# A graph layer with attention: later segment sums, earlier attention and a written-out end on TensorE

## The chip, the cores and the metric

The kernel runs on one core of a Trainium2 chip. The metric is device time of one execution in microseconds. Three executions of the kernel before took 1295.53, 1297.51 and 1299.25 us (median 1297.51). The engines are called PE (TensorE, matrix products), DVE (VectorE), ACT (ScalarE), POOL (GpSimd) and SP (SyncE, here only a queue for transfers). Each engine works through its own list of instructions in order; semaphores tie the lists together.

## What is computed

All numbers are 32-bit floats. There are 8192 nodes with 256 channels and 131072 edges, sorted by target node; the edges have 64 features.

```
ea  = edge_attr @ w_e + b_e
agg = segment_sum(relu(x[src] + ea), dst)            # the edge part
h_local = bn1(relu((x + agg) @ w1 + b1) @ w2 + b2 + x)
q, k, v = split(x @ in_w.T + in_b)                   # attention inside groups of 32 nodes, 4 heads
h_attn  = bn2(softmax(q k^T / 8) v @ out_w.T + out_b + x)
out = h_local + h_attn
out = bn3(out + relu(out @ m_w1 + m_b1) @ m_w2 + m_b2)
result = layernorm(x + out)
```

## The kernel before

The work is laid out in 264 turns, and every engine's list is written turn by turn (in each engine's block, `for turn in range(TURNS)`). Three strands run side by side.

**Edges.** An edge tile has 128 edges, a pair two tiles, a group four pairs; there are 128 groups, two turns each. For a pair POOL gathers two tiles of source rows from DRAM into one of seven slots `xg` (two indirect DMAs, L430); 14 of the 512 pairs are fetched row by row through the queues of SP and ACT instead. DVE adds the edge bias and puts the rows into one of four accumulator banks (`seed`, L681), PE adds the edge product (`products`, L867, two pairs a turn), ACT takes the relu (`message`, L469). For a group PE then sums the messages with one-hot matrices (`sum_group`, L882), ACT copies the sums (`copy_agg`, L474), PE transposes them (`transpose_agg`, L891) and DVE adds them to the 64 columns of `aggT` that belong to the group (`add_agg`, L714, four dependent adds). In DVE's list a turn begins with the seeds of the next turn's products; what stands later in the list delays the seeds of the turn after.

**Attention.** Sixteen slabs J of 512 nodes. `HEADS` and `heads_base(J)` give the turns: q and k products, scores in two halves (`sc`: PE L938, then on DVE four maxima L726 and four differences L731), the softmax halves (`soft`: exp on ACT, then DVE L738 to L747), v, and the product with v (`av`).

**Nodes.** Blocks b of nodes: twelve of 512, six of 256 (12 to 17), four of 128 (18 to 21). `NODES`, `NODES_256` and `NODES_128` give the turns of the stages w1, B (out_w and w2 in one bank), m1, m2, T (transposes back to rows, then on DVE the add of x, L779, and the statistics, L783 and L787) and y (the normalization, L792 to L803). The first 512-node block starts at turn 19, the next ones 16 turns apart. w1 of a block waits on PE until DVE has read the last T of the block before (`s_r`).

The functions that the change touches:

Of the kernel before, what the change touches and what calls it, by code (L numbers as in the profile page):

```python
# [15 lines left out]
CC = C // 128  # L16
P = 128
TG = 8
GE = TG * P
NG = E // GE  # L20
# [37 lines left out]


def heads_base(J):  # L60
    return max(16 * J - 12, 12 * J)

# [5 lines left out]
         "T": (14, 15), "log": (15, 16), "y": (16, 17), "xn": (8, 9), "out": (17, 18)}  # L68
NODES_256 = {"w1": (0,), "B": (1,), "z": (2,), "m1": (2, 3), "m2": (4,), "T": (5,), "log": (6,),
             "y": (7,), "xn": (2,), "out": (8,)}  # L70
FIRST_256 = {12: 211, 13: 217, 14: 223, 15: 229, 16: 235, 17: 243}
NODES_128 = {
# [8 lines left out]
}  # L81
LASTB = 21


SUMS = {2 * n + 1: n for n in range(NG)}
TURNS = 264
CHUNKS = {"w1": CC, "B": CC, "m1": 2 * CC, "m2": CC}

# [36 lines left out]
def nodes_in(turn, stages):  # L125
    found = []
    for b in range(len(BLOCKS)):
        if b < 12:
            plan, base = NODES, 16 * b + 19
        elif b < 18:  # L130
            plan, base = NODES_256, FIRST_256[b]
        else:
            plan, base = NODES_128[b], 0
        found += [(b, s, n) for s in stages for n, at in enumerate(plan[s]) if base + at == turn]
    return found
# [89 lines left out]
def program(nc, k):  # L225
# [3 lines left out]
    with ExitStack() as ctx:  # L229
# [88 lines left out]
        def _(sp):  # L318
# [44 lines left out]
            for turn in range(TURNS):  # L363
# [4 lines left out]
                    preload(i + AHEAD)  # L368
                if turn in (2, 12):
                    load_xT(1 if turn == 2 else 2)  # L370
                if turn % 16 == 13 and NXT <= (turn + 19) // 16 < NJ:
                    load_xT((turn + 19) // 16)
                for J, _, pair in heads_in(turn - 1, ("av",)):
                    sp.wait_ge(s_oc, 2 * J + pair + 1)
                    sp.dma_start(k.oT_dram[2 * J + pair, :, :, :],
# [458 lines left out]
        def _(pe):  # L834
# [134 lines left out]

            def node(b, stage, use):  # L970
                n0, w = BLOCKS[b]
                at, to = cols(b), bank(b, stage)
                J, of_slab = part(b)
                if stage == "w1":
                    if use:
                        pe.wait_ge(s_h1, before(b, "w1") + use)
                    else:
                        if b == 0:
                            pe.wait_ge(s_w1, 16)
                            pe.wait_ge(s_bias, 1)  # L980
                        elif b < 18:
                            pe.wait_ge(s_r, before(b, "T"))
                        elif b == 18:
                            pe.wait_ge(s_oc, 2 * NJ)
                        elif b < LASTB:
                            pe.wait_ge(s_r, before(b - 1, "T"))
                        pe.wait_ge(s_added, min((n0 + w) // PER + SLACK, NG))
                    for c, of in chunks(b, "w1", use):
                        ins = product(to[:, of], CC, lambda a: k.w1[:, a, c * P:(c + 1) * P],
                                      lambda a: aggT[:, a, n0:n0 + w])  # L990
                    ins.then_inc(s_p1, 1)
                if stage == "B":
                    early = b == LASTB
                    if use:
                        pe.wait_ge(s_o, before(b, "B") + use)
                    else:
                        pe.wait_ge(s_oc, (n0 + w + NB - 1) // NB)
                    if early:
                        for c, of in chunks(b, "B", use):
                            product(to[:, of], CC, lambda a: k.owT[:, a, c * P:(c + 1) * P],  # L1000
                                    lambda a: k.oT[:, J % NOT, a, of_slab], start=c == 0,
                                    stop=False, skip=True)
                    if not use:
                        pe.wait_ge(s_h1, before(b + 1, "w1"))
                    for c, of in chunks(b, "B", use):
                        if not early:
                            product(to[:, of], CC, lambda a: k.owT[:, a, c * P:(c + 1) * P],
                                    lambda a: k.oT[:, J % NOT, a, of_slab], stop=False)
                        ins = product(to[:, of], CC, lambda a: k.w2[:, a, c * P:(c + 1) * P],
                                      lambda a: k.h1[:, a, at], start=False, skip=early)  # L1010
                    ins.then_inc(s_p2, 1)
# [27 lines left out]
                                                      k.z[:, c, row:row + P], ident[:, :])  # L1039
                    ins.then_inc(s_t, 1)  # L1040

            for turn in range(TURNS):
                if turn < ND:
                    products(turn)
                if turn - 1 in SUMS:
                    transpose_agg(SUMS[turn - 1])
                weights(turn)
# [1 line left out]
                    attention(J, stage, n)  # L1049
                for b, stage, use in nodes_in(turn, ("T", "m2", "m1", "B", "w1")):  # L1050
                    node(b, stage, use)
                if turn in SUMS:
                    sum_group(SUMS[turn])
            with pe.If(pe.value_load(k.bad_i[0:1, 0:1], min_val=0, max_val=1) > 0):
                pe.wait_ge(s_go, 1)
                general_tensor(nc, k, g, pe)
# [309 lines left out]
```

## Time and profile before

| | |
|---|---|
| median of three executions | 1297.51 us |
| the profiled execution | 1296.03 us, of which 1294.2 us lie between its first and last instruction |
| PE / DVE / ACT / POOL busy | 89% / 64% / 42% / 73% |
| granted clock of PE, mean | 0.969 of full speed |

A busy share is an average over the span. POOL's 73% is low only because the time between two gathers does not count as busy. The chain of work that ended last runs over PE for 58% of the span, DVE for 11%, POOL for 6%.

### The profile page before, as it was taken

To read this page: it belongs to the slowest core of one execution; us is meant where nothing else is said; L and a number is where in the kernel's file an instruction comes from. 1 tells how busy PE (TensorE), PEld (TensorE's weight loads), DVE (VectorE), ACT (ScalarE), POOL (GpSimd) and SP (SyncE) were. 2 spreads that over 40 slices of the span, in tenths; PEclk is the share of its full clock that TensorE was granted. 3 is DMA by queue.
4 is the path that set the end of the run, shared out by engine and by line. 5 is a ranking of instruction groups with operands and counts; after the bars stand their busy time and mean duration, and the time that the engine had idled before them with its cause. 6 is when DMAs were issued, how large, how long until landed. Compare 5 with 4: busy or idle time off the path is not lost.

```text
span 1294.2 us, 28246 instructions
## 1 busy us (share of the span) xinstructions
PE 1154.5 (89%) x7309; PEld 647.4 (50%) x7309; DVE 826.7 (64%) x2090; ACT 541.2 (42%) x1077; POOL 944.9 (73%) x1004
## 2 busy tenths in 40 slices
PE   6787989998899899998989999998989998998896
PEld 3444454544445444444544545454444555765675
DVE  5847486767566576755758666575756667557563
ACT  1343434444344435434344443443434443443353
POOL 7777777777777777777777777777777777675770
PEclk7898999999999999999999999999999998999999
DMA  8554555655555555565555555555655565554550
GB/s 316 154 170 141 175 156 175 174 173 180 170 165 169 164 182 172 160 183 148 183 173 175 165 165 176 166 175 174 172 164 154 183 183 147 168 160 126 175 155 26
DMA packets 119282, 216.50 MB, mean 167 GB/s; under 512 B 24784, under 2 KB 69584, under 8 KB 119120
## 3 DMA queue, kind: packets, MB, share of 16 engines
q0 software_dynamic: 47808, 130.61, 35.0%
q1 hardware_dynamic: 67312, 79.47, 19.6%
q10 hardware_dynamic: 4000, 4.61, 1.0%
q8 instruction: 59, 0.97, 0.3%
q14 instruction: 103, 0.84, 0.2%
HBM read 197.82 MB, written 16.78 MB: 166 GB/s over the span
## 4 chain that ended last, share of the span: by engine, by line
PE 58%; DVE 11%; ACTq 8%; ACT 7%; issue 7%; POOL 6%; DMA 2%; DVEq 0%; SPq 0%
PE bank L837 33%; PE bank L867 12%; PE bank L882 7%; POOL xg L430 6%; ACTq L463 6%; ACT msg L469 4%; DVE bank L681 3%; PE bank L891 3%; ACTq L311 2%; DVE dif L731 2%; DVE mx L726 2%; PE bank L938 1%; DMA xT<-in_xT_dram 1%; DVE aggT L714 1%; ACT kbd L490 1%
## 5 line engine op out<-in xcount | busy, mean ns | idle before, releaser
L430 POOL DMA_INDIRECT xg<-in_x_dram,srcs x996 | 944.0, 948 | 317.4 <-issue 290.0
L469 ACT ACTIVATE msg<-bank 128x512 f32<-128x512 f32 x512 | 277.8, 595 | 543.6 <-PE bank L867 286.7
L681 DVE TENSOR_TENSOR bank<-xg,bank 128x512 f32<-128x512 f32 x498 | 327.4, 690 | 138.1 <-DMA xg<-in_x_dram,srcs 93.0
L867 PE MATMUL bank<-we,ea 64*128 64x256 f32 x2048 | 301.7, 415 | 35.5 <-DVE bank L681 35.5
L867 PEld LDWEIGHTS bank<-we,ea 64*128 64x128 f32 x2048 | 183.1, 192 | 179.7 <-issue 124.1
L714 DVE TENSOR_TENSOR aggT<-bank,aggT 128x64 f32 x512 | 115.2, 225 | 169.1 <-PE bank L891 115.2
L882 PE MATMUL bank<-msg,onehot 128*32 128x256 f32 x2048 | 141.1, 394 | 49.0 <-ACT msg L469 48.4
L837 PE MATMUL bank<-xT,iwT 128*128 128x512 f32 x256 | 128.2, 624 | 7.6 <-DMA xT<-in_xT_dram 4.0
L837 PE MATMUL bank<-o,m 128*128 128x512 f32 (+2 forms) x352 | 125.6, 491 | 4.6 <-DVE o L758 4.4
L882 PEld LDWEIGHTS bank<-msg,onehot 128*32 128x32 f32 x2048 | 54.4, 111 | 141.6 <-ACT msg L469 96.9
L837 PE MATMUL bank<-h,m 128*128 128x512 f32 (+2 forms) x352 | 116.6, 479 | 2.1 <-ACT h L529 2.1
L837 PEld LDWEIGHTS bank<-o,m 128*128 128x128 f32 x352 | 60.7, 193 | 41.3 <-issue 27.9
L837 PEld LDWEIGHTS bank<-h,m 128*128 128x128 f32 x352 | 60.0, 190 | 41.3 <-issue 34.9
L837 PE MATMUL bank<-aggT,w 128*128 128x512 f32 (+2 forms) x176 | 66.1, 510 | 15.7 <-DVE xn L779 13.8
L474 ACT COPY agg<-bank 128x256 f32<-128x256 f32 x128 | 47.5, 371 | 70.8 <-PE bank L882 67.2
L837 PEld LDWEIGHTS bank<-xT,iwT 128*128 128x128 f32 x256 | 45.4, 198 | 51.9 <-issue 46.0
L767 DVE TENSOR_TENSOR z<-bank,z 128x512 f32<-128x512 f32 (+2 forms) x44 | 23.1, 543 | 72.1 <-PE bank L837 71.9
L891 PE MATMUL bank<-ident,agg 128*128 128x128 f32 x256 | 57.7, 308 | 7.5 <-ACT agg L474 7.5
L837 PE MATMUL bank<-iwT,xT 128*128 128x256 f32 x256 | 64.3, 395 | 0.0
L837 PE MATMUL bank<-oT,owT 128*128 128x512 f32 (+2 forms) x176 | 63.6, 485 | 0.0
L529 ACT ACTIVATE h<-bank,mb 128x512 f32<-128x512 f32 (+2 forms) x88 | 47.5, 570 | 37.3 <-PE bank L837 36.9
L837 PE MATMUL bank<-h,w 128*128 128x512 f32 (+2 forms) x176 | 62.1, 476 | 0.0
(92 smaller groups left out, 938.9 us busy)
## 6 DMA issues: line engine op xcount, KB each, us to landing
rows<-in_x_dram SPq DMA_DIRECT2D x2304, 1.0 KB
ea<-in_ea_dram SPq DMA_DIRECT2D x128, 256.0 KB
rows<-in_x_dram ACTq DMA_DIRECT2D x1280, 1.0 KB
xg<-in_x_dram,srcs POOLq DMA_INDIRECT x996
xT<-in_xT_dram SPq DMA_DIRECT2D x32, 256.0 KB, 4.2
aggT<-in_xT_dram SPq DMA_DIRECT2D x32, 256.0 KB, 4.0
oT_dram<-oT SPq DMA_DIRECT2D x32, 256.0 KB
xn<-in_x_dram SPq DMA_DIRECT2D x32, 256.0 KB
```

The source lines that it names most:

```text
L311: _, of = nc.values_load_multi_w_load_instructions(k.of_rows[at:at + 1, col:col + LOADED], engines=(engine,), min_val=0, max_val=(N - 1) * ...
L430: pool.indirect_dma_start(xg[:, slot % NX, n * C:(n + 1) * C], None, t["x"], bass.IndirectOffsetOnAxis(k.srcs[:, at:at + 1], 0)).then_inc( ...
L463: act.dma_start(row_bytes[e:e + 1, row_buffer(n), two * 4 * C:(two + 1) * 4 * C], x_bytes[0:1, bass.ds(of_row[0][i % LOADED], 4 * C)]).the ...
L469: nc.scalar.activation(msg[:, q % NM, :], EA[q % 4][:, :], ACT.Relu).then_inc(s_msg, 1)
L474: nc.scalar.copy(k.agg[:, :], G[:, 0:C]).then_inc(s_agg, 1)
L529: ins = nc.scalar.activation(k.h2[:, c, at], bank(b, "m1")[:, of], ACT.Relu, bias=k.mb1[:, c:c + 1])
L681: nc.vector.tensor_tensor(EA[q % 4][:, :].rearrange("p (a c) -> p a c", a=2), pair.rearrange("p (a c) -> p a c", a=2), KB[:, 0:C].unsqueez ...
L714: nc.vector.tensor_tensor(window, sums[:, :, sub * W:(sub + 1) * W], window, ALU.add).then_inc(s_added if sub == SUB - 1 else s_part, 1)
L837: ins = nc.tensor.matmul(to, stationary(c), moving(c), start=start and c == 0, stop=stop and c == blocks - 1, skip_group_check=skip)
L867: ins = nc.tensor.matmul(EA[(2 * d + pair) % 4][:, two * C:(two + 1) * C], ea[rows, n % NEA, at:at + P], k.we[rows, :], start=False, stop= ...
L882: ins = nc.tensor.matmul(G[sub * W:(sub + 1) * W, 0:C], onehot[:, n % 2, at, :], msg[:, q % NM, two * C:(two + 1) * C], start=tile == 0, s ...
L891: ins = nc.tensor.transpose(G[:, c * P:(c + 1) * P], k.agg[:, c * P:(c + 1) * P], ident[:, :])
```

## The change

Four things are done.

1. `SUMS`: the sums of groups 0 to 113 move from the end of PE's turn 2n+1 to turn 2n+2, right behind that turn's edge products. The copy on ACT, the transposes on PE and the add on DVE follow a turn later than before. The 512-node blocks and blocks 12 to 16 start one turn later.
2. `heads_base`: attention of slabs 6 to 15 starts five turns sooner, that of slab 4 two and that of slab 5 four turns sooner. The loads of xT are issued at turn 16J-22 instead of 16J-19.
3. The last stages of blocks 19 to 21 are put on other turns on ACT and DVE, and PE's list from turn 254 on is written out.
4. The out_w half of B of block 20 becomes a step of its own ("A"), as it already was for block 21.

```diff
 def heads_base(J):
-    return max(16 * J - 12, 12 * J)
+    return max(16 * J - 17, 12 * J if J < 3 else 14 * J - 6)
...
-FIRST_256 = {12: 211, 13: 217, 14: 223, 15: 229, 16: 235, 17: 243}
+FIRST_256 = {12: 212, 13: 218, 14: 224, 15: 230, 16: 236, 17: 243}
...
+LAST_TURN = 254
...
-SUMS = {2 * n + 1: n for n in range(NG)}
+CLOSE = NG - 14
+SUMS = {(2 * n + 2 if n < CLOSE else 2 * n + 1): n for n in range(NG)}
...
-            plan, base = NODES, 16 * b + 19
+            plan, base = NODES, 16 * b + 20
...
-                if turn % 16 == 13 and NXT <= (turn + 19) // 16 < NJ:
-                    load_xT((turn + 19) // 16)
+                if turn % 16 == 10 and NXT <= (turn + 22) // 16 < NJ:
+                    load_xT((turn + 22) // 16)
...
-            for turn in range(TURNS):
-                if turn < ND:
-                    products(turn)
+            for turn in range(LAST_TURN):
+                products(turn)
+                if SUMS.get(turn, NG) < CLOSE:
+                    sum_group(SUMS[turn])
                 if turn - 1 in SUMS:
                     transpose_agg(SUMS[turn - 1])
...
-                if turn in SUMS:
+                if SUMS.get(turn, 0) >= CLOSE:
                     sum_group(SUMS[turn])
+
+            products(ND - 2)
+            transpose_agg(NG - 2)
+            node(19, "T", 0)
+            products(ND - 1)
+            node(20, "w1", 0)
+            sum_group(NG - 1)
+            node(20, "A", 0)
+            transpose_agg(NG - 1)
+            node(20, "B", 0)
+            node(LASTB, "A", 0)
+            node(LASTB, "w1", 0)
+            node(20, "m1", 0)
+            node(LASTB, "B", 0)
+            node(LASTB, "m1", 0)
+            node(20, "m2", 0)
+            node(LASTB, "m2", 0)
+            node(20, "T", 0)
+            node(LASTB, "T", 0)
```

DVE's list in the kernel before, from the first half of the scores of slab 7 (mx and dif; o is stage B of a node block, sm to probT the softmax):

```order
L726 TENSOR_REDUCE mx<-bank 32x8 x4
L731 TENSOR_TENSOR dif<-bank,mx 32x256 x4
L758 SCALAR_TENSOR_TENSOR o<-xT,s,bank 128x512
L681 TENSOR_TENSOR bank<-xg,bank 128x512 x2
L690 TENSOR_TENSOR onehot<-bank,rel 128x256
L738 TENSOR_REDUCE sm<-dif 128x8
L740 RECIPROCAL rs<-sm 128x8
L742 TENSOR_TENSOR dif<-dif,rs 128x256
L747 STREAM_TRANSPOSE probT<-dif 32x8x32 x4
```

The same place after, up to the first instruction of the normalization (lines are two higher; xn, stats and mv are stage T, fix is stage y):

```order
L728 TENSOR_REDUCE mx<-bank 32x8 x4
L733 TENSOR_TENSOR dif<-bank,mx 32x256 x4
L781 TENSOR_TENSOR xn<-bank,xn 128x512
L785 BN_STATS stats<-xn 128x6 x2
L789 BN_AGGR mv<-stats 128x2 x2
L683 TENSOR_TENSOR bank<-xg,bank 128x512
L683 TENSOR_TENSOR bank<-rows,bank 128x512
L740 TENSOR_REDUCE sm<-dif 128x8
L742 RECIPROCAL rs<-sm 128x8
L744 TENSOR_TENSOR dif<-dif,rs 128x256
L749 STREAM_TRANSPOSE probT<-dif 32x8x32 x4
L794 SCALAR_TENSOR_TENSOR fix<-root 128x2
```

Stage T of a node block now stands between the scores and the next seeds, and stage y behind the softmax; the same holds for the second half, and for every slab from 6 to 14.

PE's list in the kernel before, from the first T of node block 3 (z transposed) to the q product of slab 6:

```order
L1038 MATMUL bank<-ident,z 128x128 x4
L882 MATMUL bank<-msg,onehot 32x256 x8
L867 MATMUL bank<-we,ea 128x256 x4
L891 MATMUL bank<-ident,agg 128x128 x2
L1038 MATMUL bank<-ident,z 128x128 x4
L867 MATMUL bank<-we,ea 128x256 x4
L837 MATMUL bank<-aggT,w 128x512 x2
L882 MATMUL bank<-msg,onehot 32x256 x8
L867 MATMUL bank<-we,ea 128x256 x4
L891 MATMUL bank<-ident,agg 128x128 x2
L837 MATMUL bank<-xT,iwT 128x512 x2
```

After, from the edge products of the turn with the second T of that block (turn 83) to those of turn 86:

```order
L869 MATMUL bank<-we,ea 128x256 x4
L893 MATMUL bank<-ident,agg 128x128 x2
L940 MATMUL bank<-kbd,qT 64x128 x8
L1043 MATMUL bank<-ident,z 128x128 x4
L869 MATMUL bank<-we,ea 128x256 x4
L884 MATMUL bank<-msg,onehot 32x256 x8
L839 MATMUL bank<-aggT,w 128x512 x2
L869 MATMUL bank<-we,ea 128x256 x4
L893 MATMUL bank<-ident,agg 128x128 x2
L940 MATMUL bank<-kbd,qT 64x128 x8
L839 MATMUL bank<-aggT,w 128x512 x2
L869 MATMUL bank<-we,ea 128x256 x4
```

The sums (msg, onehot) stand right behind edge products, and the scores of slab 6 (kbd, qT) stand among the T and w1 of blocks 3 and 4.

PE's end, before, with numbers (bank5 holds block 20, bank0 to bank3 block 21), from the last sum on:

```order
L882 MATMUL bank4<-msg,onehot 32x256 x8
L891 MATMUL bank4<-ident,agg 128x128 x2
L837 MATMUL bank5<-o,m1 128x128 x8
L837 MATMUL bank0<-aggT,w1 128x128 x4
L837 MATMUL bank5<-h2,m2 128x128 x8
L837 MATMUL bank1<-oT,owT 128x128 x4
L837 MATMUL bank1<-h1,w2 128x128 x4
L1038 MATMUL bank5<-ident,z 128x128 x2
L837 MATMUL bank2<-o,m1 128x128 x8
L837 MATMUL bank3<-h2,m2 128x128 x8
L1038 MATMUL bank0<-ident,z 128x128 x2
```

After, from the oT product of block 20 on:

```order
L839 MATMUL bank5<-oT,owT 128x128 x4
L893 MATMUL bank4<-ident,agg 128x128 x2
L839 MATMUL bank5<-h1,w2 128x128 x4
L839 MATMUL bank1<-oT,owT 128x128 x4
L839 MATMUL bank0<-aggT,w1 128x128 x4
L839 MATMUL bank5<-o,m1 128x128 x8
L839 MATMUL bank1<-h1,w2 128x128 x4
L839 MATMUL bank2<-o,m1 128x128 x8
L839 MATMUL bank5<-h2,m2 128x128 x8
L839 MATMUL bank3<-h2,m2 128x128 x8
L1043 MATMUL bank5<-ident,z 128x128 x2
L1043 MATMUL bank0<-ident,z 128x128 x2
```

The out_w product of block 21 and its w1 now stand before m1 of block 20, its m1 before m2 of block 20, and both T stand at the end.

## Rows read from the trace of the kernel before

**Rows 1.** The page's group of POOL's gathers: count, busy us, mean ns, idle us.

```profile
L430 POOL DMA_INDIRECT xg<-in_x_dram,srcs x996 | 944.0, 948 | 317.4 <-issue 290.0
```

**Rows 2.** POOL's timeline near the end: start us, us, instruction, idle before.

```profile
1224.64 0.94 POOL L430 DMA_INDIRECT xg<-in_x_dram,srcs  x1 [0.30 <-issue]
...
1262.13 0.95 POOL L430 DMA_INDIRECT xg<-in_x_dram,srcs  x1 [0.30 <-issue]
```

**Rows 3.** Busy time by stretch: stretch, busy us of PE, PEld, DVE, ACT, POOL, PEclk.

```profile
422.40:966.80 544.40, 496.05 (x3024) 256.49 (x3024) 354.64 (x883) 231.79 (x449) 411.67 (x436) 0.98 0.58 170
500.60:576.60 76.00, 69.54 (x432) 35.97 (x432) 50.55 (x127) 32.43 (x63) 57.40 (x62) 1.00 0.59 172
1269.90:1294.20 24.30, 15.87 (x135) 13.63 (x134) 7.47 (x30) 7.79 (x25) 0.00 (x0) 0.98 0.06 18
112.30:115.50 3.20, 3.15 (x11) 2.15 (x12) 2.67 (x9) 1.03 (x2) 2.29 (x4) 0.50 0.63 212
```

**Rows 4.** POOL's waits from 1080 to 1200 us: total us, times, longest.

```profile
POOL xg L430 <- DVE bank L681: 13.8, 9, 3.9
```

**Rows 5.** PE's waits for messages from 422.4 to 966.8 us: total, times, longest.

```profile
PE bank L882 <- ACT msg L469: 24.1, 27, 2.4
```

**Rows 6.** DVE's timeline around turn 217: start us, us, instruction.

```profile
1078.94 0.69 DVE L779 TENSOR_TENSOR xn<-bank,xn 128x512 f32<-128x512 f32 x1
...
1080.61 1.26 DVE L681 TENSOR_TENSOR bank<-xg,bank 128x512 f32<-128x512 f32 x2
1081.79 0.42 DVE L690 TENSOR_TENSOR onehot<-bank,rel 128x256 f32<-128x256 f32 x1
1082.12 0.41 DVE L738 TENSOR_REDUCE sm<-dif 128x8 f32<-128x256 f32 x1
...
1085.08 1.29 DVE L681 TENSOR_TENSOR bank<-xg,bank 128x512 f32<-128x512 f32 x2
1086.40 1.29 DVE L714 TENSOR_TENSOR aggT<-bank,aggT 128x64 f32 x4
1087.62 1.71 DVE L726 TENSOR_REDUCE mx<-bank 32x8 f32<-32x256 f32 x4
...
1091.11 0.16 DVE L792 SCALAR_TENSOR_TENSOR fix<-root 128x2 f32<-128x2 f32 x1
...
1092.47 0.87 DVE L758 SCALAR_TENSOR_TENSOR o<-xT,s,bank 128x256 f32<-128x256 f32 x2
```

**Rows 7.** PE's timeline around turns 216 and 217.

```profile
1071.59 1.07 PE L882 MATMUL bank<-msg,onehot 128*32 128x256 f32 x16
1072.59 1.13 PE L867 MATMUL bank<-we,ea 64*128 64x256 f32 x8
1073.65 0.44 PE L891 MATMUL bank<-ident,agg 128*128 128x128 f32 x2
1074.02 1.09 PE L938 MATMUL bank<-kbd,qT 128*64 128x128 f32 x16
1075.05 0.66 PE L1038 MATMUL bank<-ident,z 128*128 128x128 f32 x4
1075.63 1.13 PE L867 MATMUL bank<-we,ea 64*128 64x256 f32 x8
1079.68 1.99 PE L837 MATMUL bank<-aggT,w 128*128 128x256 f32 x8 [2.92 <-DVE xn L779]
```

**Rows 8.** PE's timeline: edge products behind a long wait, near turn 19.

```profile
112.35 2.08 PE L867 MATMUL bank<-we,ea 64*128 64x256 f32 x8 [5.00 <-DVE bank L681]
```

**Rows 9.** PE's timeline: the edge products of turns 220 and 255, m2 of block 21.

```profile
1098.84 1.13 PE L867 MATMUL bank<-we,ea 64*128 64x256 f32 x8
...
1269.93 1.13 PE L867 MATMUL bank<-we,ea 64*128 64x256 f32 x8
...
1285.82 2.05 PE L837 MATMUL bank<-h,m 128*128 128x128 f32 x16 [1.23 <-ACT h L529]
```

**Rows 10.** PE's waits for messages from 1098.8 to 1270 us: total, times, longest.

```profile
PE bank L882 <- ACT msg L469: 4.2, 2, 3.0
```

More of the change, by code:

```diff
@@ L971, in node @@
                 n0, w = BLOCKS[b]
-                at, to = cols(b), bank(b, stage)
+                at, to = cols(b), bank(b, "B" if stage == "A" else stage)
                 J, of_slab = part(b)
@@ L991, in node @@
                     ins.then_inc(s_p1, 1)
+                if stage == "A":
+                    pe.wait_ge(s_oc, 2 * NJ)
+                    if b < LASTB:
+                        pe.wait_ge(s_h1, before(b + 1, "w1"))
+                    for c, of in chunks(b, "B", use):
+                        product(bank(b, "B")[:, of], CC,
+                                lambda a: k.owT[:, a, c * P:(c + 1) * P],
+                                lambda a: k.oT[:, J % NOT, a, of_slab], start=c == 0,
+                                stop=False, skip=True)
                 if stage == "B":
-                    early = b == LASTB
+                    early = b >= 20
                     if use:
@@ L997, in node @@
                         pe.wait_ge(s_oc, (n0 + w + NB - 1) // NB)
[L998 to L1003, printed above, removed]
                         pe.wait_ge(s_h1, before(b + 1, "w1"))
```

10 rows, old and new, of the table NODES_128 are left out of this document.

## The prediction

> **What bounds the kernel now.** I read the page's groups first, then the timelines of POOL, DVE and PE, then busy time by stretch, because the page's shares mix stages with different limits.
>
> POOL comes first. It issues 996 gathers [rows 1], and late in the run thirty of them take 1262.13 - 1224.64 = 37.49 us, 1.25 us each [rows 2]. A turn has at most four, less the 14 fetched pairs (28 of 1024 tiles), so a period of 16 turns costs POOL about 64 x 996/1024 x 1.25 = 77.8 us. From turn 83 to turn 195, seven periods, 544.4 us pass [rows 3]: 77.8 us each. So up to there POOL sets the pace and PE waits for it; a faster PE gains nothing there. In one whole period at full clock (turns 99 to 115, 76.0 us) PE is busy 69.54 us [rows 3], so about 8 us of each 77.8 are free.
>
> Later the 256-node blocks make PE's list denser. POOL then waits for free slots nine times in 1080 to 1200 us, 13.8 us in all [rows 4]; each wait holds the usual 0.30 us between two gathers [rows 2], so about 11 us are lost. That is all that POOL's pace could give back. Behind the last edge products (turn 255, at 1269.93) come 24.3 us of which PE is busy 15.87 [rows 3, 9].
>
> **The sums behind the next turn's products.** No instruction is added. In turns 83 to 195 PE waited for messages before a sum 24.1 us in 27 waits [rows 5]; these go. It is worth nothing there by itself, since POOL's pace hides it; cover gone, it would count. What is new: a sum waits for the add of the group before, which DVE does right behind the seeds (1.22 us from its start to the next start [rows 6]) while PE spends 1.06 on products [rows 7], so up to about 0.3 us; and ACT copies a group's sums behind its other work of that turn, while PE's transposes come 1.06 us of products later. The trace of before has no copy in that place. I bound this by nothing and by 0.6 us at three of the eight transposes of a period (an estimate from the copy's new place behind a second ACT operation; 1.8 a period), and take nothing, since the products lie beside it; the end is kept for the range.
>
> **Attention five turns sooner, node blocks one turn later.** This is the term that decides. Attention and blocks shift by six turns against each other. For slabs 6 to 14 the first score half now falls into the turn of the second T of a block, the second half two turns on into that of the second y, as the DVE list in the section on the change shows. Durations of these pieces, as distances between starts [rows 6]: T 1.67, two seeds 1.18 (1.32 ahead of the add), onehot 0.33, softmax half 2.96, add 1.22, score half 3.49, y 1.36.
>
> DVE's list from the first T (end of turn 2 of a period, counted from a multiple of 16) to the seeds of turn 7 is: T 1.67, seeds 1.32, add 1.22, onehot 0.33, scores 3.49, T 1.67, seeds 1.18, softmax 2.96, y 1.36, seeds 1.32, add 1.22, onehot 0.33, scores 3.49, y 1.36, seeds 1.18: 24.1 us. Nothing in it can start before PE has done that T, right ahead of turn 3's products, and turn 7's products need its end. In POOL's pace four turns take 19.5 us. PE's own work in these four turns is four products 4.24, two sums 2.00, two transposes 0.74, two score steps 2.06, a T 0.58 and two w1 3.9 [rows 7]: 13.5. In before the score halves stand eight to ten turns into a period, where no T and no y stands.
>
> The other twelve turns of a period keep PE's remaining work, 69.54 - 13.5 = 56.0 us, in order behind turn 7's products. So a period is at least 24.1 + 56.0 = 80.1 us, 2.3 above POOL's pace, and POOL's seven slots only postpone this: the lag adds up.
>
> To this comes the clock. Turn 7's products wait about 5 us for seeds (scores, y and seeds of DVE against a sum of PE). Near turn 19 the trace has this very wait: 5.00 us, then eight product records in 2.08 us instead of 1.13 [rows 7, 8], and a granted clock of 0.50 over the next 3.2 us [rows 3], the 1.2 GHz level. At half speed 3.2 us do 1.6 us of work, so the period becomes 81.7. The lower end is no loss (after 2.92 us of waiting the w1 of rows 7 ran at full speed), the upper 3.2 for a second such stretch at w1, which waits about 3 us for T behind the scores; that one lies beside DVE's list, so I take one.
>
> The Trainium skill, "TensorE: Matmul & The Clock Gate", section "HAM oscillation — how this bites in real kernels", says that a wait which recurs before each piece of work starts every piece at half clock, so the price is paid each time. The trace agrees for one such wait [rows 3, 8]; by the rule the period is the 81.7 above, without it 80.1.
>
> From turn 83 (422.4 us [rows 3], taken unchanged, as POOL sets it; two us either way, since the turns just before become denser) to turn 211 are eight periods: 8 x 81.7 = 653.6, so 1076.0. Before, eight periods of POOL would be 622.
>
> **From turn 211 on.** Before, the crowding already stands at slabs 14 and 15 (turns 216 and 232): rows 6 and 7 are from it. After, it stands at turns 211 and 227. The first costs 24.1 us plus the stage-B operation of block 12, 0.87 [rows 6]: 25.0 to turn 215. Before, turn 220 to 255 took 1269.93 - 1098.84 = 171.1 [rows 9]. After, turn 215 to 255 is the same sequence plus five turns and one 256-node block: products 5.3, 2.5 sums with transposes 3.4, 56 records of w1, B, m1 and m2 at 1.99/8 us 13.9, T 0.6 [rows 7], together 23.2. One of the two waits for messages (4.2 in all, the longer 3.0 at a sum that keeps its place [rows 10]) goes: -1.2. So 193.1, and turn 255 is at 1076.0 + 25.0 + 193.1 = 1294.1.
>
> **The end.** The same products in another order. The wait of 1.23 us before m2 of block 21 [rows 9] goes, as m2 of block 20 now stands there; both T then queue on DVE one after the other. Bounds: nothing, and all of 24.3 - 15.87 = 8.4 us of idle time [rows 3]; I take 1.2, the row that the new order touches: 23.1 us.
>
> **Edits at nothing.** xT is issued three turns sooner in SP's queue and lands five turns ahead of its use; it waits for stage B made one turn before, and the edge features queued behind it are two groups ahead. That covers a turn of waiting; without the cover it would be a turn, 4.9 us, per slab. Gathers are unchanged.
>
> **Sum.** 1294.1 + 23.1 = 1317.2 us span; the profiled run has 1296.03 - 1294.2 = 1.8 around it: 1319.0. It lies 1.5 below the median of three, which is noise of the runs; I predict 1319.
>
> **Rivals.**
> *Faster: the denser late stage loses work to the slack of the earlier one.* For it: 8 us free in each period and 24.1 us of waits removed. Then POOL's lost 11 us and 1.2 at the end come back: 1296.0 - 12.2 = 1284. Against it: a wait of PE behind DVE's list is not filled by slack elsewhere in the period, because PE works in order. It needs DVE's 24.1 us not to stand between turns 3 and 7. Chance 0.10. The Trainium skill, "Perfetto Trace Analysis", section "Optimization Strategy", says that interleaving stages whose limiting engine differs can improve time; that is this case, and no row here shows it.
> *About the same: the crowding costs only its bare length.* No clock loss (80.1 a period: 1063.2 at turn 211), and with attention five turns sooner the late waits fall away, about 8 us of those 193.1: 1063.2 + 25.0 + 185.1 + 23.1 + 1.8 = 1298. Chance 0.08.
> *Much slower: every transfer between lists turns late.* A second half-clock stretch (1.6) and transposes behind ACT's copies (1.8) make 85.1 a period, 27 us more: 1346. Against it: both lie beside other work. Chance 0.08.
> *The change does not do what it says*: the lists show that it does; no chance of its own.
>
> **How the numbers follow.** The forecast has 0.74: 1319, by its bounds 1304 (half of the clock loss, 5 us less late) to 1334 (1.8 a period for the copies). About 0.3%, 4 us, is what a measurement here tells from no change. Faster: the first rival and a little of the second, 0.12; same: most of the second, 0.07; slower 0.81. The range from 1298 to 1336 leaves out the first rival and the last.
>
> **What would show it.** In the profile after: a period of 81 to 82 us from turn 83 on instead of 77.8; PE waiting some 5 us for seeds once a period with half clock behind it, and some 3 us for T before w1; DVE without a gap for 24 us there; POOL waiting for slots from the middle of the run; hardly a wait for messages before turn 229. Wrong it would be if periods stay at 77.8, or if the second score half does not hold back turn 7's seeds.

## The result and the profile after

The changed kernel takes 1357.86 us (median of four executions, 1356.22 to 1359.08), the kernel before, beside it, 1297.89: a ratio of 1.0463 [1.0444, 1.0483], 60 us slower. The forecast said slower, 1319 us, in a range up to 1336. The direction came out, and so did the mechanism of the eight middle periods; three terms of the sum did not.

The span grew from 1294.2 to 1354.5 us. Split at the edge products of turns 83, 211 and 255, first the kernel before, then after (stretch, its length, busy us and records of PE, PEld, which is PE's weight loads, DVE, ACT and POOL, then granted clock, DMA share, GB/s):

```profile
422.40:1042.30 619.90, 567.02 (x3458) 292.74 (x3458) 405.29 (x1009) 265.25 (x513) 468.86 (x496) 0.98 0.58 170
1042.30:1269.90 227.60, 206.63 (x1424) 143.68 (x1424) 141.44 (x379) 98.65 (x218) 158.57 (x168) 0.97 0.52 155
```

```profile
437.90:1104.80 666.90, 579.94 (x3457) 299.85 (x3456) 399.67 (x1008) 264.10 (x513) 469.37 (x496) 0.96 0.53 158
1104.80:1331.40 226.60, 203.66 (x1408) 142.28 (x1406) 140.60 (x378) 94.66 (x213) 152.38 (x161) 0.95 0.52 151
1331.40:1354.50 23.10, 16.21 (x143) 14.43 (x142) 9.01 (x37) 8.56 (x27) 0.00 (x0) 0.96 0.06 19
```

Turn 83 comes 15.5 us later, the eight periods up to turn 211 take 47.0 more, the late stage 1.0 less, the end 1.2 less (23.1 against the 24.3 of [rows 3]): 60.3 together. In the eight periods DVE is busy for 6 us less than before, and only 60% of the time. Still it is DVE that now sets the pace of four turns in every sixteen. The page's busy shares and the chain of work that ended last, after:

```profile
PE 1174.6 (87%) x7309; PEld 658.3 (49%) x7309; DVE 818.9 (60%) x2090; ACT 538.1 (40%) x1077; POOL 944.2 (70%) x1004
...
PE 57%; DVE 21%; ACTq 7%; issue 6%; ACT 4%; POOL 2%; DMA 2%; SPq 1%; DVEq 1%
```

All of these busy shares are lower than before, yet DVE's share of the chain is 21%, where it was 11%. DVE's timeline in the period that begins at 605.21 us (start us, us, instruction, in brackets the idle time before it):

```profile
605.31 0.69 DVE L781 TENSOR_TENSOR xn<-bank,xn 128x512 f32<-128x512 f32 x1 [2.52 <-PE bank L1043]
...
609.70 1.71 DVE L728 TENSOR_REDUCE mx<-bank 32x8 f32<-32x256 f32 x4
611.44 1.72 DVE L733 TENSOR_TENSOR dif<-bank,mx 32x256 f32<-32x256 f32 x4
613.19 0.69 DVE L781 TENSOR_TENSOR xn<-bank,xn 128x512 f32<-128x512 f32 x1
...
622.97 1.71 DVE L728 TENSOR_REDUCE mx<-bank 32x8 f32<-32x256 f32 x4
624.72 1.72 DVE L733 TENSOR_TENSOR dif<-bank,mx 32x256 f32<-32x256 f32 x4
...
627.83 1.29 DVE L683 TENSOR_TENSOR bank<-xg,bank 128x512 f32<-128x512 f32 x2
629.03 0.41 DVE L740 TENSOR_REDUCE sm<-dif 128x8 f32<-128x256 f32 x1
```

Brackets stand for idle times of 0.15 us and more. Behind the first row none has one, in the rows left out neither: the list runs without such a gap from the first T to the seeds of turn 7, 605.31 to 629.03. PE's timeline beside it:

```profile
605.21 1.13 PE L869 MATMUL bank<-we,ea 64*128 64x256 f32 x8
...
613.94 1.98 PE L839 MATMUL bank<-aggT,w 128*128 128x512 f32 x4 [3.12 <-DVE xn L781]
...
629.17 2.08 PE L869 MATMUL bank<-we,ea 64*128 64x256 f32 x8 [5.23 <-DVE bank L683]
...
643.06 0.44 PE L893 MATMUL bank<-ident,agg 128*128 128x128 f32 x2 [0.58 <-ACT agg L476]
```

From turn 3's products (605.21) to turn 7's (629.17) 24.0 us pass; it is 24.0 in seven of the eight periods and 24.2 in the first. Before, the four turns took 22.9 us on average (20.1 to 26.2), hardly less. What changed is PE's share in them: the sums over the eight stretches from turn 3 to turn 7, then over the eight from turn 7 to the next turn 3, before:

```profile
sum 183.12, PE 166.12 PEld 75.72 DVE 99.10 ACT 85.72 POOL 138.93; mean PE 20.76 PEld 9.47 DVE 12.39 ACT 10.71 POOL 17.37
sum 436.75, PE 400.87 PEld 216.98 DVE 306.17 ACT 179.49 POOL 329.91; mean PE 50.11 PEld 27.12 DVE 38.27 ACT 22.44 POOL 41.24
```

And after:

```profile
sum 192.05, PE 118.16 PEld 62.76 DVE 178.09 ACT 75.50 POOL 121.58; mean PE 14.77 PEld 7.85 DVE 22.26 ACT 9.44 POOL 15.20
sum 474.91, PE 461.83 PEld 237.10 DVE 221.59 ACT 188.66 POOL 347.80; mean PE 57.73 PEld 29.64 DVE 27.70 ACT 23.58 POOL 43.47
```

PE's work moved out of four turns that DVE's list holds at 24 us (20.8 busy us became 14.8) into twelve turns that it now fills (50.1 became 57.7, and their length 54.6 became 59.4).

The 5.23 us wait ends in eight records at half the usual speed, 2.08 us. Busy time by stretch shows the level behind it:

```profile
629.20:631.30 2.10, 2.10 (x9) 1.27 (x10) 1.97 (x6) 0.00 (x1) 1.49 (x3) 0.50 0.41 121
```

0.50 is the 1.2 GHz level. After the shorter wait at w1, 3.12 us, this period's w1 ran at full speed (1.98 us). PE's waits over the eight periods (total us, times, longest), before:

```profile
PE bank L882 <- ACT msg L469: 25.5, 29, 2.4
PE bank L867 <- DVE bank L681: 16.9, 18, 2.8
PE bank L891 <- ACT agg L474: 5.1, 8, 0.6
PE bank L837 <- DVE xn L779: 4.7, 7, 0.8
```

And after:

```profile
PE bank L869 <- DVE bank L683: 45.8, 14, 5.2
PE bank L839 <- DVE xn L781: 25.0, 8, 3.1
PE bank L893 <- ACT agg L476: 14.2, 28, 0.7
PE bank L884 <- ACT msg L471: 1.7, 3, 0.9
```

The waits for messages nearly went, as the change had it; those for seeds (L867, in the changed kernel L869), for T and for the copied sums stood there before and grew. All in all PE waits some 34 us more. The other 13 of the 47 are its busy time for the same work (567.0 to 579.9): the mean granted clock fell from 0.98 to 0.96. POOL, which set the pace before, now waits for slots. Its waits from turn 83 to turn 211, before and then after:

```profile
POOL xg L430 <- DVE bank L681: 6.7, 22, 0.3
```

```profile
POOL xg L432 <- DVE bank L683: 60.3, 47, 6.7
```

### The profile page after: what moved, and what is told of

Its sections match the earlier page's. It is cut to its first block, busy times and chain, and to the rows that moved or that the text cites. A ratio compares the mean times of both kernels' runs of the same rounds, so it can differ in the third digit from the quotient of the medians.

```text
span 1354.5 us, 28248 instructions
## 1 busy us (share of the span) xinstructions
PE 1174.6 (87%) x7309; PEld 658.3 (49%) x7309; DVE 818.9 (60%) x2090; ACT 538.1 (40%) x1077; POOL 944.2 (70%) x1004
## 4 chain that ended last, share of the span: by engine, by line
PE 57%; DVE 21%; ACTq 7%; issue 6%; ACT 4%; POOL 2%; DMA 2%; SPq 1%; DVEq 1%
PE bank L839 35%; PE bank L869 11%; PE bank L884 6%; ACTq L465 5%; DVE bank L683 5%; DVE mx L728 4%; DVE dif L733 3%; PE bank L893 3%; DVE aggT L716 2%; POOL xg L432 2%; PE bank L966 2%; ACTq L313 2%; DVE probT L749 2%; ACT msg L471 1%; DMA xT<-in_xT_dram 1%
## 5 line engine op out<-in xcount | busy, mean ns | idle before, releaser
L869 PE MATMUL bank<-we,ea 64*128 64x256 f32 x2048 | 309.3, 423 | 86.6 <-DVE bank L683 84.0
L683 DVE TENSOR_TENSOR bank<-xg,bank 128x512 f32<-128x512 f32 x498 | 319.0, 689 | 102.1 <-ACT msg L471 77.9
L869 PEld LDWEIGHTS bank<-we,ea 64*128 64x128 f32 x2048 | 187.0, 196 | 245.3 <-issue 119.0
L839 PE MATMUL bank<-xT,iwT 128*128 128x512 f32 x256 | 125.4, 613 | 2.6 <-DMA xT<-in_xT_dram 2.6
L839 PE MATMUL bank<-aggT,w 128*128 128x512 f32 (+2 forms) x176 | 71.6, 544 | 29.4 <-DVE xn L781 29.0
L769 DVE TENSOR_TENSOR z<-bank,z 128x512 f32<-128x512 f32 (+2 forms) x44 | 23.1, 544 | 106.4 <-PE bank L839 106.4
L839 PE MATMUL bank<-iwT,xT 128*128 128x256 f32 x256 | 73.6, 438 | 0.0
L893 PEld LDWEIGHTS bank<-ident,agg 128*128 128x128 f32 x256 | 27.2, 149 | 79.1 <-ACT agg L476 59.8
L760 DVE SCALAR_TENSOR_TENSOR o<-xT,s,bank 128x512 f32<-128x512 f32 (+2 forms) x44 | 25.5, 599 | 60.9 <-PE bank L839 60.8
```

What stands on the lines that cost most here:

```text
L683: nc.vector.tensor_tensor(EA[q % 4][:, :].rearrange("p (a c) -> p a c", a=2), pair.rearrange("p (a c) -> p a c", a=2), KB[:, 0:C].unsqueez ...
L839: ins = nc.tensor.matmul(to, stationary(c), moving(c), start=start and c == 0, stop=stop and c == blocks - 1, skip_group_check=skip)
L869: ins = nc.tensor.matmul(EA[(2 * d + pair) % 4][:, two * C:(two + 1) * C], ea[rows, n % NEA, at:at + P], k.we[rows, :], start=False, stop= ...
L893: ins = nc.tensor.transpose(G[:, c * P:(c + 1) * P], k.agg[:, c * P:(c + 1) * P], ident[:, :])
```

## The experiments

The theory: DVE's crowded list between turns 3 and 7, the half clock behind it, and ScalarE's late copies set the period; turn 83's lateness has a cause of its own. All runs stand in one table. The kernel before took 1296.68, 1297.49 and 1295.88 us beside the first four, the next four and the last two; the turns are where their edge products start in the profiled run, and "gather" is where POOL starts the first gather for turn 83's products (the 327th of 996 in every run).

| run | median us | ratio to before | gather | turn 83 | turn 211 | turn 255 | span |
|---|---|---|---|---|---|---|---|
| before | | | 413.4 | 422.4 | 1042.3 | 1269.9 | 1294.2 |
| after | 1357.86 | 1.0463 [1.0444, 1.0483] | 421.9 | 437.9 | 1104.8 | 1331.4 | 1354.5 |
| e1 attention only | 1322.69 | 1.0211 [1.0188, 1.0235] | 415.7 | 430.3 | 1071.0 | 1294.1 | 1319.3 |
| e2 sums only | 1305.63 | 1.0066 [1.0049, 1.0083] | 423.4 | 435.3 | 1058.0 | 1279.8 | 1304.0 |
| e3 end only | 1294.06 | 0.9972 [0.9956, 0.9987] | 415.3 | 425.3 | 1045.1 | 1269.6 | 1292.8 |
| e4 copy first | 1332.62 | 1.0273 [1.0256, 1.0291] | 418.1 | 432.6 | 1088.0 | 1311.2 | 1334.4 |
| e5 light scores | 1323.51 | 1.0221 [1.0168, 1.0273] | 422.5 | 438.6 | 1081.8 | 1298.8 | 1322.0 |
| e6 late slabs, 227 | 1287.5 | 0.993 [0.9903, 0.9958] | 415.6 | 424.4 | 1048.1 | 1263.3 | 1286.5 |
| e7 early sums old | 1350.99 | 1.0409 [1.0382, 1.0437] | 418.6 | 435.7 | 1102.5 | 1327.0 | 1350.1 |
| e8 late slabs, 225 | 1290.32 | 0.9957 [0.9937, 0.9976] | 413.1 | 422.1 | 1045.7 | 1264.5 | 1287.5 |
| e9 node blocks only | 1303.7 | 1.0061 [1.0038, 1.0084] | 415.6 | 428.6 | 1058.2 | 1277.0 | 1301.2 |
| e10 all uncrowded | 1286.77 | 0.9929 [0.9911, 0.9947] | 416.9 | 427.4 | 1051.4 | 1263.2 | 1286.4 |

A single turn 83 is known to some 3 us: e3, e6 and e8 have the early turns of the kernel before unchanged and stand at +2.9, +2.0 and -0.3. The gather's start in them is +1.8, +2.1 and -0.3.

**The three parts alone.** Each is put into the kernel before: e1 the attention and the loads of xT, e2 the sums with the node blocks a turn later, e3 the written-out end.

```diff
 # e1, in the kernel before
-    return max(16 * J - 12, 12 * J)
+    return max(16 * J - 17, 12 * J if J < 3 else 14 * J - 6)
...
-                if turn % 16 == 13 and NXT <= (turn + 19) // 16 < NJ:
+                if turn % 16 == 10 and NXT <= (turn + 22) // 16 < NJ:
```

> The kernel before with attention (and the xT loads) moved as in the change, the sums and node blocks left where they were. Theory of the crowding (scores, T and y of DVE meet only where both shifts act together): here the first score half stands a turn behind the second T, DVE's list from it to the seeds of turn 7 is about 18 us, a period of 16 turns stays near POOL's 77.8 us, turn 211 comes near 1042 us, and the whole takes 1285 to 1300 us. Rival, attention five turns sooner costs by itself: 1335 to 1360 us with periods of 82 us and more. Rival, both parts cost by themselves and add up: about 1328 us.

It took 1322.69, which none of the cases gave. Attention alone costs 26 us, without the node blocks' turn. Of the 25.1 us of span, 7.9 lie before turn 83 and 20.8 in the eight periods, where a period is 80.1 us; behind turn 211, 4.5 come back (part of the 7.9, see below). PE's waits there (430.3 to 1071.0):

```profile
PE bank L882 <- ACT msg L469: 31.9, 26, 3.0
PE bank L867 <- DVE bank L681: 22.8, 14, 3.3
PE bank L938 <- ACT kbd L490: 8.3, 5, 1.8
```

Here the first score half stands ahead of a y instead of a T, and the second among seeds and softmax halves. The seeds are late, so the messages are, and the sum at the turn's end waits for those. So the scores need no T beside them to cost time. But DVE's list is not the only cause here: 8.3 us are waits for ScalarE's copies of k (kbd), of which the kernel before has none in these periods, and no run separates the two.

```diff
 # e2, in the kernel before
-FIRST_256 = {12: 211, 13: 217, 14: 223, 15: 229, 16: 235, 17: 243}
+FIRST_256 = {12: 212, 13: 218, 14: 224, 15: 230, 16: 236, 17: 243}
-SUMS = {2 * n + 1: n for n in range(NG)}
+CLOSE = NG - 14
+SUMS = {(2 * n + 2 if n < CLOSE else 2 * n + 1): n for n in range(NG)}
...
-            plan, base = NODES, 16 * b + 19
+            plan, base = NODES, 16 * b + 20
```

> The kernel before with the sums of groups 0 to 113 behind the next turn's products and the node blocks a turn later, attention and the end left where they were. Theory of the crowding: the waits for messages before a sum go, the transposes wait for ACT's copies instead (up to 2 us a period), both inside the 8 us that POOL leaves free: periods of 77.8 us, 1295 to 1306 us in all. Rival, the later sums cost by themselves (copies of ACT, adds and one-hots in one turn of DVE): 1335 to 1360 us, with turn 83 already some 15 us late as in the changed kernel. Rival, both parts add up: about 1328 us.

It took 9 us more, the upper end of what the theory allowed, with part of what the rival had said, a late turn 83 (+12.9). From there to turn 211 a period is 77.8 us, POOL's pace as before. So what the sums and the node blocks' turn cost lies where POOL's pace was thought to hide it.

```diff
 # e3, in the kernel before: blocks 19 to 21 and PE's list from turn 254 on as in the change; the sums of before
+CLOSE = 0
+SUMS = {(2 * n + 2 if n < CLOSE else 2 * n + 1): n for n in range(NG)}
```

> The kernel before with the written-out end alone (stages of blocks 19 to 21 on their new turns). Prediction's term: 1.2 us less behind the last edge products (23.1 instead of 24.3 us), so 1296.5 to 1297.5 us; the rows of the changed kernel already show 23.1 us from turn 255's products to the end. Rival, the new turns of ACT and DVE hold something up in turns 254 to 263 that the late kernel hid: 1298 us or more.

It gained 2.6 us, more than the 1.2 of the term; the tail behind turn 255 took 23.2 us instead of 24.3, and the rest is not explained. The parts add up to 26 + 9 - 2.6 = 32 us; together they cost 60. In the eight periods it is 20.8 + 2.8 - 0.1 = 23.5 against 47.0: attention and node blocks cost more in common than apart, as the forecast had it, but not only in common.

**The copy.** In e4 ScalarE copies the closed group right behind the turn's messages, ahead of q, k and stage B of that turn.

```diff
 # e4, in the changed kernel, ScalarE's list
+                if SUMS.get(turn, NG) < CLOSE:
+                    copy_agg(SUMS[turn])
...
-                if turn in SUMS:
+                if SUMS.get(turn, 0) >= CLOSE:
```

> The changed kernel, but ACT copies a group's sums (of groups 0 to 113) right behind its messages instead of behind its attention and node work of that turn. Theory that the 1.7 us a period above 81.7 are transposes waiting for that copy: PE's waits for it (14.2 us in 437.9 to 1104.8 us) fall to near nothing, a period falls from 83.4 to about 81.8 us, the early turns gain some 3 us, in all 1338 to 1346 us. Rival, the waits only move to the next instruction (ACT's other work is then late by the copy): 1353 to 1359 us.

25 us came back, more than the 12 to 20 expected. The profiled runs show 20.1 of them (that of e4 is the longest of its four, that of the change the shortest): 5.3 before turn 83, 11.5 in the periods, 3.4 behind turn 211. ScalarE's timeline after, at the transposes of 643.06 above:

```profile
641.45 0.58 ACT L503 COPY qT<-bank 128x512 f32<-128x512 f32 x1 [1.83 <-PE bank L839]
...
641.93 0.81 ACT L525 ACTIVATE z<-o,c,s 128x512 f32<-128x512 f32 x1
...
642.65 0.36 ACT L476 COPY agg<-bank 128x256 f32<-128x256 f32 x1
```

The copy stands behind a q copy and an activation that works on stage B's result (z), and PE's transposes wait 0.58 us for it. In e4's periods PE's waits are above all these two, and none for copies of sums:

```profile
PE bank L871 <- DVE bank L685: 37.0, 8, 5.3
PE bank L841 <- DVE xn L783: 26.2, 8, 3.3
```

The turns 3 to 7 still take 24.0 us, and a period is 81.9: the 81.7 of the forecast, which had left the copies out. Of the 14.2 us that PE waited for copies in the changed kernel, 2.9 lie in turns 3 to 7, beside DVE's list, where they cost nothing; 11.3 lie in the twelve other turns, and 11.5 is what e4 gains in the periods.

**The list.** In e5 three of the four score differences of each half are left out from slab 6 on, so the probabilities of these slabs are not the reference's.

```diff
 # e5, in the changed kernel, DVE
-                    for m, g in enumerate(quarter):
+                    for m, g in enumerate(quarter if J < 6 else quarter[:1]):
```

> The changed kernel with three of the four score differences on DVE left out for slabs 6 to 15, so the attention of these slabs is not computed: 1.3 us less in each of the two score steps of DVE's list between the first T and turn 7's seeds. Theory (that list alone sets the time from turn 3's to turn 7's products): 24.0 us become 21.4, a period 83.4 becomes 80.8, some 21 us less up to turn 211 and 2 to 3 after it, in all 1331 to 1338 us. Rival (PE, ACT or POOL set that time and the list only looks busy): 24 us stay, 1352 to 1359 us.

Turns 3 to 7 went from 24.0 to 21.0 us, and the eight periods from 666.9 to 643.2: 3.0 us each, a little more than the 2.6 expected. The late stage became 9.6 us shorter where 2 to 3 were expected, so the whole lies below the theory's 1331. The waits for seeds and for T fell (to 40.7 in 24 waits and 13.5 in 8). One of the shortened pieces:

```profile
617.62 0.41 DVE L733 TENSOR_TENSOR dif<-bank,mx 32x256 f32<-32x256 f32 x1
617.97 0.14 DVE L794 SCALAR_TENSOR_TENSOR fix<-root 128x2 f32<-128x2 f32 x1
```

Start to start the differences take 0.35 us, where 626.47 - 624.72 = 1.75 stood: 2 x 1.40 = 2.8 us less in DVE's list. What is taken from the list comes off these turns and the period in full, so the list is what sets these turns.

**Turn 83.** First theory: the early sums behind the next products make the start late. e7 puts the sums of the first 42 groups back.

```diff
 # e7, in the changed kernel
+OPEN = 42
+BEHIND = range(OPEN, CLOSE)
-SUMS = {(2 * n + 2 if n < CLOSE else 2 * n + 1): n for n in range(NG)}
+SUMS = {(2 * n + 2 if n in BEHIND else 2 * n + 1): n for n in range(NG)}
```

> The changed kernel, but the sums of groups 0 to 41 (up to turn 83) stay at the end of turn 2n+1 as before; later ones stand behind the products. Theory that the later sums make turn 83 late (in slabs 0 to 2 the add, the one-hot, a score half and a softmax half then fall into one turn of DVE): turn 83 comes at 424 to 430 instead of 437.9 us and the whole takes 1343 to 1350 us. Rival, the q and k products of slab 6 and the closer slabs 4 to 6 make it late: turn 83 stays at 435 us or more and the whole at 1353 to 1359 us.

Turn 83 stayed at 435.7, as the rival had it, and the whole lies between the two cases. What e7 and e2 share are the node blocks a turn later, so e9 has these alone.

```diff
 # e9, in the kernel before
-FIRST_256 = {12: 211, 13: 217, 14: 223, 15: 229, 16: 235, 17: 243}
+FIRST_256 = {12: 212, 13: 218, 14: 224, 15: 230, 16: 236, 17: 243}
-            plan, base = NODES, 16 * b + 19
+            plan, base = NODES, 16 * b + 20
```

> The kernel before with one edit alone: each slab's node blocks begin one turn later (base 16b + 20, and the first 256-wide slab's one turn later too). Sums and attention stand as before. Theory: the later node blocks are what the runs with late turn 83 have in common (435.3 with the sums behind the next turn, 435.7 with the early sums put back), so turn 83 should start at 430 to 437 us and the whole take 1298 to 1306. Rival: the later node blocks cost nothing alone, turn 83 at 422 to 427 us and the whole at 1294 to 1300; then the later sums and the earlier attention each make the start late by a way of their own and hide one another's cost.

Turn 83 fell between the two, at 428.6 (+6.2), with the whole time of the theory, 1303.7. The shifts of e9 (6.2) and e1 (7.9) add up to the 13.3 of e7, but e1's 7.9 are no loss of that size. In e1 and in the changed kernel the four q and k products of slab 6 stand ahead of turn 83's products; before, they stand behind them. Busy time from turn 19 to turn 83, before:

```profile
112.30:422.40 310.10, 287.73 (x1778) 150.84 (x1778) 199.69 (x497) 132.58 (x254) 234.18 (x249) 0.98 0.57 169
```

The same in e1 and in the changed kernel, then in e1 PE's q and k products alone (tile iwT) over the last 20 us ahead of turn 83:

```profile
112.20:430.30 318.10, 295.88 (x1794) 155.38 (x1794) 200.36 (x500) 136.66 (x261) 238.24 (x252) 0.98 0.56 167
111.60:437.90 326.30, 301.15 (x1790) 157.42 (x1790) 197.31 (x491) 134.32 (x260) 239.38 (x253) 0.96 0.55 164
410.00:430.30 20.30, 7.73 (x16) 1.00 0.49 137
```

e1 has sixteen records more, these four products, 7.7 us of PE's time; in the kernel before none stands in those 20 us. PE is busy for 8.2 us more and idle as long as before (22.2 us, 22.4 then). So this work only changed sides at turn 83; sixteen such records, those of slab 14, are missing from turn 211 on.

POOL's list shows what was really lost, since it has the same gathers in the same order in every run. Its gather for turn 83, before and then after:

```profile
413.43 0.95 POOL L430 DMA_INDIRECT xg<-in_x_dram,srcs  x1 [0.30 <-issue]
```

```profile
421.87 0.94 POOL L432 DMA_INDIRECT xg<-in_x_dram,srcs  x1 [0.30 <-issue]
```

It starts 8.4 us later after the change, and 9.9 in e2. In e1 and e9 it is 2.3 and 2.1, hardly more than in e3 and e6, whose early turns are those of before. With the copies in front it is 4.7 (e4) and 3.5 (e10), with the early sums at their old place 5.2 (e7). So the first theory was right about part of what POOL lost: it goes with the later sums, and above all with their copies at the back of ScalarE's turn (6.4 us between e2 and e10, 3.7 between the changed kernel and e4). The other 7.1 us of turn 83's 15.5 fit the four products. (e9's loss comes later: its gather for turn 211 is 10.7 us late.)

**Without the crowding.** Late slabs 13 to 15 stood among the T of 256-node blocks already in the kernel before. e6 has the new end and moves these three slabs alone; e8 puts the last one two turns earlier.

```diff
 # e6, in the kernel of e3 (e8: 15: 225)
-    return max(16 * J - 12, 12 * J)
+    return {13: 195, 14: 209, 15: 227}.get(J, max(16 * J - 12, 12 * J))
```

> The kernel before with the written-out end (as in the run of the end alone, 1294 us) and three slabs moved: slab 13 at 195, slab 14 at 209, slab 15 at 227, so that no score half falls into a turn with T or B of a 256-node block. Theory of the crowding: PE's waits for T (2.9 and 4.2 us) and for B (3.6 us) near turns 217, 219 and 235 go or shrink to 2 us, with them the half clock behind them, and POOL loses less than its 11 us: 1281 to 1289 us. Rival, those waits were covered by POOL or come back elsewhere: 1292 to 1297 us.

> As the run before it, with slab 15 at 225: its softmax halves, not its scores, then fall into the turns of B and of the second m1 of block 15. Theory of the crowding: B's result is late by a softmax half (3 us), T is free: 1283 to 1291 us, within 3 us of the run with 227. Rival, no gain from either: 1292 to 1297 us.

e6 takes 1287.5, below both kernels and in the range of its theory. Turns 211 to 255 went from 227.6 to 215.2 us. PE's waits for T and for stage B in the late stage (from 1040 us to turn 255), before and then in e6, which has 0.4 us for stage B:

```profile
PE bank L837 <- DVE xn L779: 7.7, 3, 4.2
...
PE bank L837 <- DVE o L758: 3.9, 2, 3.6
```

```profile
PE bank L839 <- DVE xn L781: 1.7, 1, 1.7
```

The waits for T are mostly gone. e8 takes 1290.32, in its range too; the intervals of the two overlap.

e10 keeps the later sums, the node blocks' turn and the new end of the change, puts the copy in front, and takes attention back, with slab 14 two turns earlier than before.

```diff
 # e10, in the kernel of e4; the loads of xT as before
-    return max(16 * J - 17, 12 * J if J < 3 else 14 * J - 6)
+    return {13: 196, 14: 210, 15: 228}.get(J, max(16 * J - 12, 12 * J))
```

> The changed kernel with ScalarE's copy of the closed group right behind the messages and with attention back at its old turns but for the last three slabs (196, 210 and 228): the later sums and the written-out end remain. Crowding theory: turn 3 to turn 7 of a period back to 18 us, no term of the earlier attention left, so 1358 less some 60 to 70: 1285 to 1300. If the later sums bring anything of their own once nothing is crowded, it comes out below 1284; if they cost by themselves (waits of the next turn's products, later node blocks), 1295 to 1306, above the kernel before with the late slabs moved (1287.5). Rival: the cost of the change does not lie in the crowding by attention, and the time stays above 1320.

1286.77, the level of e6: taking back attention's turns, moving the copy and moving slab 14 give back all 60 us, and the run is 9 us below the kernel before. The three were not parted. Nor does e10 tell what the later sums bring, since the node blocks' turn, which costs 8 us alone (e9), is in it too. In the eight periods there is no gain. PE's largest waits from 425 to 1045 us in e10, and its busy time from turn 83 to turn 211:

```profile
PE bank L871 <- DVE bank L685: 41.5, 21, 3.2
```

```profile
427.40:1051.40 624.00, 577.46 (x3461) 300.18 (x3460) 403.97 (x1008) 264.64 (x513) 472.05 (x499) 0.96 0.57 170
```

The kernel before waited there for messages (25.5 us) and seeds (16.7), 42.2 in all; now the seeds alone take 41.5, in 21 waits instead of 46. With the smaller ones all waits are 52.2 us before and 44.6 in e10. PE's busy time grew in turn, from 567.0 to 577.5 us for nearly the same work at a granted clock of 0.96 instead of 0.98. POOL waits for slots as before (6.7 us in 22 waits), and the periods take 624.0 us against 619.9: under POOL's pace what PE gains in one place it waits for, or loses to its clock, in another.

## Why the prediction was wrong

Its sum was 1317.2 us of span; the trace has 1354.5. By its terms:

- **Turns 3 to 7, 24.1 us a period: right.** 24.0 measured, the list without a gap as worked out from [rows 6], and e5 shows that its length is what counts.
- **The half clock, 1.6 us once a period: right.** Turn 7's products take 2.08 us instead of 1.13 in each of the eight periods, and PE is busy for 57.7 us in the twelve turns, where the forecast had 56.0 + 1.6. The second stretch, at w1, came in five of the eight and lay beside DVE's list, as the forecast had argued. The rule that I cited from the Trainium skill, "TensorE: Matmul & The Clock Gate", section "HAM oscillation — how this bites in real kernels", that a recurring wait costs the clock each time, is borne out by the wait at turn 7, in all eight periods. The wait at w1 recurs as regularly, 3.12 us each time, and cost the clock in five.
- **"I bound this by nothing and by 0.6 us at three of the eight transposes of a period ... and take nothing, since the products lie beside it": failed, 13.3 us.** The period is 666.9 / 8 = 83.4, not 81.7. Measured is the upper bound: 14.2 us of waits for copies over eight periods is 1.8 each, and e4, without them, has 81.9. The products do not cover the copy: ScalarE copies after q, k and z of the turn, and these become ready late.
- **"422.4 us, taken unchanged, as POOL sets it; two us either way": failed, 15.5 us, the largest miss.** It failed twice. POOL did not keep its pace: its gather for turn 83 comes 8.4 us late, with the later sums and their copies as the main cause that the runs show (e2, e10, e4), the term taken at nothing. And the four q and k products of slab 6, which the change puts ahead of turn 83, are in no stage of the forecast's sum: the stretch up to turn 83 was left as it was, and the one from turn 211 on was counted without those of slab 14. They make some 7 us. How much of the 8.4 is noise of a single run (2 us in e3 and e6) stays open.
- **Turn 211 to 255, 25.0 + 193.1 us: 8.5 short.** 27.4 to turn 215, where PE waits 3.01 us for a stage-B operation (o) of DVE and then runs m1 and the edge products at half speed, and 199.1 behind it. Two waits for edge features from SP's queue make 2.5; a late SP queue was in the forecast at nothing. Moving the copies gives back 3.4 (e4), though PE waits for them only 1.3 us here: its busy time falls from 203.7 to 199.3, with the clock at 0.98 instead of 0.95. The rest was not split further.
- **The end, 23.1 us: right, in part by luck.** The 1.23 us wait is gone and e3 has 23.2. But w1 of block 20, 1.06 us, now stands behind turn 255's products, which the forecast did not count, and other small waits went that it had not named.

15.5 + 13.3 + 8.5 = 37.3, all of the gap. The copies and POOL's early pace have one kind: a term was taken at its lower bound because something was thought to cover it. The q and k products are another: work that crosses the line between two stages of the sum. The lower bound of 1304 does not follow from its own terms, which give 1319 - 6.4 - 5 = 1308; nothing hangs on it here.

The rival "every transfer between lists turns late" (1346) was the nearest, and had 0.08; its copies came in full, its second half-clock stretch cost nothing that shows. The two rivals that spoke of gain and of no change are out. The claim that "attention and blocks shift by six turns against each other" decides was right in the crowded list but too narrow: five turns alone cost 26 us (e1).

## What to carry to other kernels

An engine at 60% busy can set the pace: add up what stands in its list between two of its handovers, not over the span, and compare with the pace there. Where an operation is moved behind others on an engine, take the wait that it makes at its upper bound unless a row shows the cover, and do so in every stage that the edit reaches, the early ones too. When a sum is split at a turn, list the work that the edit moves across it; an instruction stream that is the same in both kernels, as POOL's gathers here, is a better clock than an edited one. A wait removed under a pace that another engine sets gained nothing here (e10's periods: 624.0 us against 619.9); the gain lay where that pace did not hold, in the last fifty turns.

## What the runs showed of the hardware

TensorE's half level came after the waits of 5.1 to 5.2 us at turn 7, in all eight periods. The wait at w1 is 3.12 us long in every period, behind the same instructions; the half level followed it in five periods and not in three. One of the five (w1 takes 3.65 us, where the period shown above has 1.98), and a wait of 3.01 us at turn 214, from the timeline of after:

```profile
529.97 3.65 PE L839 MATMUL bank<-aggT,w 128*128 128x512 f32 x4 [3.12 <-DVE xn L781]
...
1128.56 3.78 PE L839 MATMUL bank<-o,m 128*128 128x256 f32 x8 [3.01 <-DVE o L760]
1132.27 2.08 PE L869 MATMUL bank<-we,ea 64*128 64x256 f32 x8
```

So neither the length of a wait nor the instructions just ahead of it told here whether it costs the clock.
